# Maxima of a cross-attention kernel: rounds of four in four banks instead of three in three

## The chip, the cores and the metric

The kernel runs on one core of one Trainium2 chip. The metric is the device time of one execution in microseconds (us): the median of three runs of the kernel before is 1541.65 us, and they lie between 1541.1 and 1544.61 us. The engines are called PE (TensorE, matrix products), PEld (its weight loads), DVE (VectorE), ACT (ScalarE), POOL (GpSimd) and SP (which issues most of the transfers).

## The reference, cut to what matters

The inputs are x (4 x 2048 x 640) and ctx (4 x 154 x 384). The last four rows of each ctx are the tokens `ca`, the first 150 the keys.

```
query = x @ Wq;  keyt = enc @ Wk;  valt = enc @ Wv
hs = _mha(query, keyt, valt)                          # 8 heads, 2048 x 150
ca_q1 = jnp.einsum('btc,th->bch', ca, Wq_ca)          # 384 x 640
ca_q1 = ca_q1[:, indices, :]                          # 384 rows spread over 2048
ca_hs1 = _mha(ca_q1, residual, residual)              # 384 distinct rows against all 2048 rows of x
ca_q2 = ca_hs1 @ Wq
ca_hs2 = _mha(ca_q2, ca @ Wk_ca, ca @ Wv_ca)
out = (hs + ca_hs2) @ Wout + b_out + residual
```

The change is in `ca_hs1`. Its scores are a product of rank 4 in each head: `g` = x times `Wq_ca` by head (4 rows a head) against the 384 columns of `ca`. Softmax needs the greatest score of each of the 384 rows, and the kernel computes it over all 2048 positions before it computes any exponential.

## The kernel before

The program loops over four batches, and each goes through the same stages, written out by hand for each engine; semaphores join the engines.

**Stage of products.** x comes in four chunks of 512 rows, each in five column blocks, so 20 pieces m = 0..19. For each piece PE transposes four 128x128 blocks into a PSUM bank (`turn_x`), ACT copies the bank to `xt` (`copy_x`), and PE multiplies the copy with `gyw_b` (`products`, 8 matmuls as the profile shows them). After the five pieces of a chunk, ACT and DVE take the sums (`copy_y`), DVE splits the token columns (`split_g`), PE turns them (`turn_g`) and ACT copies them to `g` (`copy_g`). The pieces and the turned `g` alternate between the two banks of `ps_t` (`piece_bank`, `piece_free`). In the same stage PE also computes the first chunk's queries for the main attention, 75 matmuls of 512 columns, in portions of `Q0_FILL` per step and then of `Q0_SPLIT`, `Q0_TURNED` and `Q0_TRIPLE` (`queries0`).

**Maxima.** A unit (`max_unit`) is one matmul of 12 or 28 rows by 512 columns: one group r (0..3, two heads, rows from 32 r) of one of three blocks of 128 rows against one chunk. Each fills a bank of `ps_s`, and DVE reduces that bank to 128 maxima (`unit_maxima`, L1311). There are 48 units for the even heads (phase 0) and 48 for the odd heads (phase 1). `UNITS_EARLY` says how many units of phase 1 run in the stage of products beside the 48 of phase 0: 6 in each of chunks 0 and 1, which makes 60. They come in 20 groups of three (`TRIPLES`, then the last four groups with five query matmuls between them). With three banks, unit u waits until DVE has reduced unit u - 3. The PE stream is in order: behind a unit that waits, everything of PE waits. `TRIPLES[m]` puts a group after the transposes, after the products or after the queries of step m.

**First softmax phase.** After the 60 units DVE puts the maxima in place (`place_maxima`), PE turns them into bank 2 of `ps_s` (`turn_ca`, T_BANK), and DVE copies that to `ca_mat` (`take_ca`, L1327). Then come 16 steps: scores (`scores`, rows 0 to 63 into `ps_w`, rows 64 to 127 into `ps_t`), ACT's exponentials (L1124) and weighings (`weigh`). The other 36 units stand between the scores, `UNITS_STEP` of them a step, in three banks.

The second softmax phase and 16 tiles of the main attention follow, and are the same in both kernels.

Of the kernel before, what the change touches and what calls it, by code (L numbers as in the profile page):

```python
# [21 lines left out]
P = 128  # L22
# [101 lines left out]
M_BANKS = 3  # L124
# [4 lines left out]
UNITS_EARLY = 6  # L129


def unit_order():

    early, late = [], []
    for q in range(CHUNKS):
        units = [(ct, r) for ct in range(CT) for r in range(GROUPS)]
        early += [(0, q, ct, r) for ct, r in units]
        n = UNITS_EARLY if q + 2 < CHUNKS else 0
        early += [(1, q, ct, r) for ct, r in units[:n]]
        late += [(1, q, ct, r) for ct, r in units[n:]]  # L140
    return early + late, len(early)
# [4 lines left out]
TRIPLES = {8: (AFTER_TURNED, AFTER_QUERIES), 9: (AFTER_PRODUCTS,), 10: (AFTER_TURNED,), 11: (AFTER_TURNED,), 12: (AFTER_TURNED,),  # L146
           13: (AFTER_TURNED, AFTER_QUERIES), 14: (AFTER_PRODUCTS,), 15: (AFTER_TURNED,), 16: (AFTER_TURNED,), 17: (AFTER_TURNED,),
           18: (AFTER_TURNED, AFTER_QUERIES), 19: (AFTER_PRODUCTS,), 20: (AFTER_TURNED,)}
UNITS_BEFORE_SPLIT = 12
Y_SHARED = (0,)  # L150
Q0_FILL = [0] * 6 + [3, 0, 4, 3, 2, 1, 2, 4, 4, 2, 2, 3, 4, 4, 1]
Q0_ENDS = (6, 12, 17)
Q0_SPLIT, Q0_TURNED, Q0_TRIPLE = 9, 3, 5
UNITS_STEP = [3, 2, 3, 2, 3, 2, 2, 3, 2, 3, 2, 3, 2, 2, 0, 0]
# [65 lines left out]
def cross_attention(nc, x, ctx, Wq, Wk, Wv, Wq_ca, Wk_ca, Wv_ca, Wout, b_out,  # L220
                    c_ident, c_head_of, c_block_of, c_pick, c_rem_of, c_last_row, c_hi_lo, c_spread, out):
    with ExitStack() as stack:
# [167 lines left out]
        piece_bank = {piece: ps_t[:, n % 2, :] for n, piece in enumerate(PIECES)}  # L390
# [115 lines left out]
        def _(pe):  # L506
# [80 lines left out]
            for b in range(B):  # L587
# [16 lines left out]
                for n in V_ORDER:  # L604
                    if n == 1:
                        pe.wait_ge(ca_base_ready, PHASES * (b + 1))
                    if n == V_ORDER[-1]:
                        pe.wait_ge(xc_in[0], 16 * (b * XC_LOADS + 1))
                        turn_x(0, 0, piece_bank[("x", 0)], gx_turned)
# [35 lines left out]
                def turn_g(i):  # L645
# [3 lines left out]
                    for t in range(ST):  # L649
                        last = turned(piece_bank[("g", i)][:, t * P:(t + 1) * P], gst[:, t, :, :].rearrange("p h k -> p (h k)"))  # L650
# [39 lines left out]
                for m in range(GX + 1):  # L690
                    if 0 < m < GX:
# [22 lines left out]
                    triple(AFTER_PRODUCTS)  # L714
# [3 lines left out]
                    triple(AFTER_QUERIES)  # L718
# [5 lines left out]
                for u in range(first, PHASE0_UNITS, M_BANKS):  # L724
                    max_units(u, M_BANKS)
                    if u + M_BANKS < PHASE0_UNITS:
                        queries0(done, Q0_TRIPLE)
                        done += Q0_TRIPLE
# [245 lines left out]
        def _(act):  # L974
# [22 lines left out]
            for b in range(B):  # L997
# [12 lines left out]
                def copy_x(m):  # L1010
# [10 lines left out]
                    nc.scalar.activation(xt[:, xt_slot(m), :], piece_bank[("x", m)], copy).then_inc(xt_copied, 1)  # L1021
# [157 lines left out]
        def _(dve):  # L1179
# [77 lines left out]
            for b in range(B):  # L1257
# [82 lines left out]
                for i in range(1, CHUNKS):  # L1340
                    chunk = per_chunk + (UNITS_EARLY if i < CHUNKS - 1 else 0)
# [177 lines left out]
```

## Time and profile before

| | |
|---|---|
| median of three runs | 1541.65 us (1541.1 to 1544.61) |
| the profiled execution | 1540.79 us |
| its span, first to last instruction | 1539.0 us |
| mean granted TensorE clock | 0.996 |
| busy: PE, PEld, DVE, ACT | 97%, 81%, 51%, 40% |
| PE's share of the chain that ended last | 91% |

Busy shares are averages over unlike stages. PE's rows overlap each other, and their ends are modelled; what a piece of work costs PE is the distance from its start to the start of what comes next. An "idle before" value says how long the engine stood still, and for whom. A wait that sits between two matmuls of one group is inside the group's duration, so a group's second number is to be compared with that of its like.

### The profile page before, as it was taken

The numbers are of one execution on the slowest core, as the hardware profiler recorded it, in microseconds if no ns is written. First come the engines' busy times: TensorE is split into PE (matmuls) and PEld (weight loads), VectorE is DVE, ScalarE is ACT, GpSimd is POOL, SyncE is SP. The second block draws the span as 40 slices with busy tenths as digits, with TensorE's granted clock in tenths as the row PEclk, the third lists the DMA queues.
The fourth block names the chain that finished last, engine by engine and source line by source line (L and its number), as shares of the span: only waits on it lengthen the run. The fifth ranks groups of instructions, "written<-read, shape, count | busy, mean of one in ns | idle before, by whom it ended". The sixth has DMA issues, their size and how long they took to land.

```text
span 1539.0 us, 24550 instructions
## 1 busy us (share of the span) xinstructions
PE 1499.8 (97%) x10306; PEld 1247.5 (81%) x10306; DVE 791.1 (51%) x1595; ACT 620.0 (40%) x1310; POOL 2.8 (0%) x12
## 2 busy tenths in 40 slices
PE   6999999999999999999999999999999999999998
PEld 4764699999976489999987549999998745999998
DVE  5686445344468453443447826335345882443533
ACT  1428723233243862332333584233333368333322
POOL 0000000000000000000000000000000000000000
PEclk9999999999999999999999999999999999999999
DMA  6530011130253001131035200204004510021101
GB/s 241 205 136 35 3 54 70 55 114 26 89 170 130 1 16 48 66 111 54 35 111 182 88 1 20 82 28 156 18 35 155 180 38 1 20 95 57 61 18 43
DMA packets 46680, 117.28 MB, mean 76 GB/s; under 512 B 3661, under 2 KB 5317, under 8 KB 45019
## 3 DMA queue, kind: packets, MB, share of 16 engines
q1 hardware_dynamic: 37036, 93.91, 17.4%
q10 hardware_dynamic: 9535, 21.80, 3.7%
q8 instruction: 82, 1.34, 0.3%
q14 instruction: 27, 0.22, 0.0%
HBM read 77.33 MB, written 39.17 MB: 76 GB/s over the span
## 4 chain that ended last, share of the span: by engine, by line
PE 91%; DVE 4%; ACT 2%; issue 2%; DMA 0%; SPq 0%
PE ps_w L508 46%; PE ps_s L508 19%; PE ps_t L508 16%; PE ps_t L518 5%; PE ps_w L518 3%; DVE unit_max L1311 2%; ACT work L1124 1%; PE ps_s L518 1%; ACT ot L1038 0%; DMA y_all<-in_L_xattn_Wv_ca_dram 0%; DVE ca_mat L1327 0%; DVE ot L1423 0%; ACT ot L1107 0%; DVE xt_l L1337 0%; ACT work L1021 0%
## 5 line engine op out<-in xcount | busy, mean ns | idle before, releaser
L508 PE MATMUL ps_w<-wo_h,ot 128*128 128x320 f32 x1280 | 310.4, 314 | 0.6 <-DVE ot L1423 0.6
L1311 DVE TENSOR_REDUCE unit_max<-ps_s 128x1 f32<-128x512 f32 x384 | 240.6, 683 | 53.1 <-PE ps_s L508 52.2
L1094 ACT ACTIVATE work<-ps_s,neg_max 128x150 f32<-128x150 f32 x512 | 152.5, 403 | 223.4 <-DVE neg_max L1369 223.4
L508 PEld LDWEIGHTS ps_w<-wo_h,ot 128*128 128x128 f32 x1280 | 220.3, 188 | 0.9 <-DVE ot L1423 0.9
L508 PE MATMUL ps_w<-wo_l,ot 128*128 128x320 f32 x640 | 197.4, 308 | 0.0
L508 PEld LDWEIGHTS ps_w<-v_all,work 120*128 120x128 f32 x1280 | 170.3, 190 | 3.0 <-issue 2.5
L508 PE MATMUL ps_w<-v_all,work 120*128 120x162 f32 (+1 forms) x1280 | 171.3, 288 | 0.0
L1365 DVE TENSOR_REDUCE neg_max<-ps_s 128x6 f32<-128x900 f32 x64 | 70.1, 1095 | 165.2 <-PE ps_s L508 165.2
L508 PE MATMUL ps_s<-keys_h,qt_h 128*128 128x300 f32 (+1 forms) x448 | 140.0, 313 | 0.0
L508 PE MATMUL ps_s<-keys_h,qt_l 128*128 128x300 f32 (+1 forms) x448 | 131.5, 294 | 0.0
L508 PE MATMUL ps_s<-keys_l,qt_h 128*128 128x300 f32 (+1 forms) x448 | 131.1, 293 | 0.0
L1434 DVE TENSOR_TENSOR work<-ps_w,xc 128x320 f32<-128x320 f32 x128 | 62.4, 488 | 130.9 <-PE ps_w L508 130.9
L1391 DVE TENSOR_TENSOR qt_l<-ps_t,qt_h 128x512 fp32r<-128x512 f32 x60 | 41.5, 691 | 162.1 <-ACT qt_h L1076 162.1
L508 PEld LDWEIGHTS ps_w<-wo_l,ot 128*128 128x128 f32 x640 | 120.4, 188 | 0.2
L508 PE MATMUL ps_t<-xt_h,wq_h 128*128 128x512 f32 x300 | 119.3, 398 | 0.4
L1124 ACT ACTIVATE work<-ps_w 128x768 f32<-128x768 f32 x128 | 104.2, 814 | 35.2 <-PE ps_t L508 20.8
L508 PE MATMUL ps_t<-xt_h,wq_l 128*128 128x512 f32 x300 | 117.7, 392 | 0.0
L508 PE MATMUL ps_t<-xt_l,wq_h 128*128 128x512 f32 x300 | 116.6, 389 | 0.0
L1107 ACT ACTIVATE ot<-ps_w 128x640 fp32r<-128x640 f32 x64 | 45.0, 704 | 175.1 <-PE ps_w L518 175.1
L508 PE MATMUL ps_w<-work,y_all 128*32 128x384 f32 x1024 | 109.1, 498 | 0.1
L508 PEld LDWEIGHTS ps_s<-keys_h,qt_h 128*128 128x128 f32 x448 | 84.9, 189 | 25.5 <-issue 25.0
L1076 ACT ACTIVATE qt_h<-ps_t 128x512 fp32r<-128x512 f32 x60 | 35.9, 598 | 169.3 <-PE ps_t L508 169.3
(163 smaller groups left out, 2346.9 us busy)
## 6 DMA issues: line engine op xcount, KB each, us to landing
xc<-in_x_dram SPq DMA_DIRECT2D x32, 1280.0 KB, 6.5
out_dram<-work ACTq DMA_DIRECT2D x64, 320.0 KB, 2.2
xt_all<-work SPq DMA_DIRECT2D x60, 256.0 KB, 2.2
xt_l<-xt_all SPq DMA_DIRECT2D x12, 1280.0 KB, 5.6
y_all<-in_L_xattn_Wk_dram SPq DMA_DIRECT2D x4, 960.0 KB
y_all<-in_L_xattn_Wv_dram SPq DMA_DIRECT2D x4, 960.0 KB
pick<-pick_all SPq DMA_DIRECT2D x16, 194.0 KB
xc<-in_L_xattn_Wq_dram SPq DMA_DIRECT2D x1, 1600.0 KB, 10.5
```

Source lines behind the costliest of these rows:

```text
L508: return nc.tensor.matmul(out, lhs, rhs, start=start, stop=stop, skip_group_check=True)
L518: return nc.tensor.transpose(out, in_, ident[0:k, 0:k])
L1076: nc.scalar.activation(dst, ps_t[:, bank_of(use), :], copy).then_inc(t_high, 1)
L1094: return nc.scalar.activation(probs[:, h * KEYS:(h + 1) * KEYS], ps_s[:, bank, c * KEYS:(c + 1) * KEYS], exp, bias=neg_max[:, s % 2, h:h + ...
L1107: nc.scalar.activation(ot_h[:, s % 2, :], ot_psum, copy).then_inc(ot_high, 1)
L1124: nc.scalar.activation(e_buf[n % E_BUFS][:, 2 * p:2 * p + 2, :], score_banks[p], exp, scale=SCALE).then_inc(w_ready, 1)
L1311: v.tensor_reduce(unit_max[:, a, n, q:q + 1], bank, AX_X, ALU.max).then_inc(max_free, 1)
L1365: v.tensor_reduce(neg_max[:, s % 2, 0:6].rearrange("p (a h) -> p a h", a=2), ps_s[:, 0:2, 0:3 * KEYS].rearrange("p a (h k) -> p a h k", h= ...
L1391: v.tensor_tensor(dst, ps_t[:, bank_of(use), :], high_part, ALU.subtract).then_inc(t_free[bank_of(use)], 1)
L1434: v.tensor_tensor(o_tile[:, s % 2, cols], out_banks[half], xc[:, c % 2 * ST + t, cols], ALU.add).then_inc((ya_ready, y_ready)[half], 1)
```

## The change

The maxima of the stage of products run four at a time in four banks: the three of `ps_s` and the second bank of `ps_t`. That bank had been half of the pair in which the turned pieces alternate, so all pieces now use the first bank of `ps_t`, and each waits for the copy of the one before. `UNITS_EARLY` becomes 4 and 4, so 56 units run in the stage of products, in 14 rounds of four (11 by `ROUNDS`, then three with five queries between), and 40 are left for the first softmax phase, which keeps its three banks. The queries' portions are dealt out anew: the three at m = 6, which ran ahead of the products, go to later steps, and 14 instead of 9 stand between the last round and `turn_ca(0)`. Unit 56, the first of the softmax phase, now falls into bank 2, the one that `turn_ca` has just filled, and so waits for `ca_ready`; the number of throwaway matmuls (`UNREAD`) is as before, with another bank.

```diff
-M_BANKS = 3
+M_BANKS, G_BANKS = 3, 4
-UNITS_EARLY = 6
+UNITS_EARLY = [4, 4, 0, 0]
-        n = UNITS_EARLY if q + 2 < CHUNKS else 0
+        n = UNITS_EARLY[q]
-TRIPLES = {8: (AFTER_TURNED, AFTER_QUERIES), 9: (AFTER_PRODUCTS,), 10: (AFTER_TURNED,), 11: (AFTER_TURNED,), 12: (AFTER_TURNED,),
-           13: (AFTER_TURNED, AFTER_QUERIES), 14: (AFTER_PRODUCTS,), 15: (AFTER_TURNED,), 16: (AFTER_TURNED,), 17: (AFTER_TURNED,),
-           18: (AFTER_TURNED, AFTER_QUERIES), 19: (AFTER_PRODUCTS,), 20: (AFTER_TURNED,)}
+ROUNDS = {8: AFTER_TURNED, 9: AFTER_TURNED, 10: AFTER_TURNED, 12: AFTER_PRODUCTS, 13: AFTER_TURNED,
+          14: AFTER_TURNED, 15: AFTER_TURNED, 17: AFTER_PRODUCTS, 18: AFTER_TURNED, 19: AFTER_TURNED, 20: AFTER_TURNED}
+UNIT_BANK = [u % (G_BANKS if u < PHASE0_UNITS else M_BANKS) for u in range(PHASES * UNITS)]
+UNIT_PREVIOUS = [max((w for w in range(u) if UNIT_BANK[w] == UNIT_BANK[u]), default=None) for u in range(PHASES * UNITS)]
-Q0_FILL = [0] * 6 + [3, 0, 4, 3, 2, 1, 2, 4, 4, 2, 2, 3, 4, 4, 1]
-Q0_ENDS = (6, 12, 17)
-Q0_SPLIT, Q0_TURNED, Q0_TRIPLE = 9, 3, 5
-UNITS_STEP = [3, 2, 3, 2, 3, 2, 2, 3, 2, 3, 2, 3, 2, 2, 0, 0]
+Q0_FILL = [0] * 7 + [4, 3, 2, 2, 2, 2, 4, 3, 2, 3, 3, 4, 3, 2]
+Q0_ENDS = (12, 17)
+Q0_SPLIT, Q0_TURNED, Q0_ROUND = 9, 3, 5
+UNITS_STEP = [3, 3, 3, 2, 3, 3, 3, 2, 3, 3, 3, 3, 3, 1, 0, 0]
-        piece_bank = {piece: ps_t[:, n % 2, :] for n, piece in enumerate(PIECES)}
+        piece_bank = ps_t[:, 0, :]
+        unit_banks = [ps_s[:, 0, :], ps_s[:, 1, :], ps_s[:, 2, :], ps_t[:, 1, :]]
                 def piece_free(piece):
-                    if n >= 2:
-                        kind, old = PIECES[n - 2]
+                    if n:
+                        kind, old = PIECES[n - 1]
                 def max_unit(u):
-                    if u >= M_BANKS:
-                        pe.wait_ge(max_free, b * PHASES * UNITS + u - M_BANKS + 1)
+                    if u >= G_BANKS:
+                        pe.wait_ge(max_free, b * PHASES * UNITS + UNIT_PREVIOUS[u] + 1)
-                queries0(done, 2 * Q0_TRIPLE)
+                queries0(done, KT * Q0_MM)
                 turn_ca(0)
-                queries0(done + 2 * Q0_TRIPLE, KT * Q0_MM)
-                    mm(ps_s[:, T_BANK, :], wq_h[:, n, 0:P], xt_h[:, n, :], True, True)
+                    mm(unit_banks[UNIT_BANK[PHASE0_UNITS + 2]], wq_h[:, n, 0:P], xt_h[:, n, :], True, True)
-                    chunk = per_chunk + (UNITS_EARLY if i < CHUNKS - 1 else 0)
+                    chunk = per_chunk + UNITS_EARLY[i - 1]
```

## Rows read from the trace of the kernel before

**Rows 1.** The page: the chain that ended last, by engine.
```profile
PE 91%; DVE 4%; ACT 2%; issue 2%; DMA 0%; SPq 0%
```
**Rows 2.** Busy time by window: us, PE, PEld, DVE, ACT, POOL, clock, DMA.
```profile
438.60:490.20 51.60, 50.34 (x297) 35.94 (x297) 42.38 (x76) 13.93 (x26) 0.00 (x0) 1.00 0.44 148
...
494.30:515.90 21.60, 21.60 (x188) 8.84 (x187) 18.96 (x31) 18.62 (x26) 0.00 (x0) 1.00 0.02 8
...
849.50:852.90 3.40, 3.40 (x13) 2.92 (x13) 1.93 (x6) 0.98 (x2) 0.00 (x0) 0.51 0.90 322
```
**Rows 3.** PE in order of time, second batch: start, duration, instruction, count, idle before.
```profile
437.21 0.60 PE L518 MATMUL ps_t<-ident,gst 128*128 128x128 f32 x4
437.65 0.60 PE L518 MATMUL ps_t<-ident,xc 128*128 128x128 f32 x4
438.59 0.50 PE L508 MATMUL ps_s<-ot,ca_mat 12*128 12x512 f32 x3 [0.34 <-ACT ot L1038]
439.02 1.10 PE L508 MATMUL ps_w<-gyw_b,work 128*128 128x56 f32 x8
...
441.04 0.50 PE L508 MATMUL ps_s<-ot,ca_mat 12*128 12x512 f32 x3
...
442.92 1.09 PE L508 MATMUL ps_s<-ot,ca_mat 12*128 12x512 f32 x3
...
445.81 1.10 PE L508 MATMUL ps_w<-gyw_b,work 128*128 128x56 f32 x8
...
459.70 0.60 PE L518 MATMUL ps_t<-ident,xc 128*128 128x128 f32 x4
460.23 0.50 PE L508 MATMUL ps_s<-ot,ca_mat 12*128 12x512 f32 x3
460.66 1.10 PE L508 MATMUL ps_w<-gyw_b,work 128*128 128x56 f32 x8
```
**Rows 4.** DVE in order of time: six reductions behind two groups of units.
```profile
441.58 3.76 DVE L1311 TENSOR_REDUCE unit_max<-ps_s 128x1 f32<-128x512 f32 x6 [0.60 <-PE ps_s L508]
```
**Rows 5.** ACT in order of time: the copy of g and the copy of a chunk's sums.
```profile
437.85 0.60 ACT L1038 ACTIVATE ot<-ps_t 128x512 fp32r<-128x512 f32 x1 [0.70 <-PE ps_t L518]
...
446.94 0.98 ACT L1033 ACTIVATE y_all<-ps_w 128x448 f32<-128x448 f32 x2 [0.97 <-PE ps_w L508]
```
**Rows 6.** PE in order of time: the end of the stage and the first scores.
```profile
480.46 0.50 PE L508 MATMUL ps_s<-ot,ca_mat 12*128 12x512 f32 x3
...
482.25 1.14 PE L508 MATMUL ps_s<-ot,ca_mat 12*128 12x512 f32 x3
...
489.76 0.49 PE L518 MATMUL ps_s<-ident,cst 128*128 128x128 f32 x3
490.18 0.50 PE L508 MATMUL ps_s<-ot,ca_mat 28*128 28x512 f32 x2
490.90 0.44 PE L508 MATMUL ps_w<-ca_mat,ot 32*128 32x384 f32 x2 [0.22 <-DVE ca_mat L1327]
```
**Rows 7.** PE in order of time: steps 6 and 7 of the stage of products.
```profile
433.48 0.48 PE L508 MATMUL ps_w<-xt_h,wq_h 128*128 128x512 f32 x1
...
435.00 1.07 PE L508 MATMUL ps_w<-gyw_b,work 128*128 128x56 f32 x8 [0.57 <-DVE y_all L1294]
435.91 0.61 PE L518 MATMUL ps_t<-ident,xc 128*128 128x128 f32 x4
436.36 1.02 PE L508 MATMUL ps_w<-gyw_b,work 128*128 128x84 f32 x8
```
**Rows 8.** DVE in order of time in the first softmax phase.
```profile
495.59 7.87 DVE L1311 TENSOR_REDUCE unit_max<-ps_s 128x1 f32<-128x512 f32 x12 [0.78 <-PE ps_s L508]
```
**Rows 9.** PE in order of time: the start of a step of the first softmax phase.
```profile
495.06 0.50 PE L508 MATMUL ps_s<-ot,ca_mat 28*128 28x512 f32 x1
495.06 0.44 PE L508 MATMUL ps_w<-ca_mat,ot 32*128 32x384 f32 x2
495.07 0.49 PE L508 MATMUL ps_s<-ot,ca_mat 28*128 28x512 f32 x1
```

More of the change, by code:

```diff
@@ L411, in unit @@
         def unit(u):
-            return (*UNIT_ORDER[u], ps_s[:, u % M_BANKS, :])
+            return (*UNIT_ORDER[u], unit_banks[UNIT_BANK[u]])
         @block.sync
@@ L608, in _ @@
                         pe.wait_ge(xc_in[0], 16 * (b * XC_LOADS + 1))
-                        turn_x(0, 0, piece_bank[("x", 0)], gx_turned)
+                        turn_x(0, 0, piece_bank, gx_turned)
                     at, lo, hi = KR * n % KEYS, V_HEADS[n][0] * DH, (V_HEADS[n][-1] + 1) * DH
@@ L649, in turn_g @@
                     for t in range(ST):
-                        last = turned(piece_bank[("g", i)][:, t * P:(t + 1) * P], gst[:, t, :, :].rearrange("p h k -> p (h k)"))
+                        last = turned(piece_bank[:, t * P:(t + 1) * P], gst[:, t, :, :].rearrange("p h k -> p (h k)"))
                     last.then_inc(gt_full, 1)
@@ L697, in _, with a_round @@
                         piece_free(("x", m))
-                        turn_x(i % 2, kt, piece_bank[("x", m)], gx_turned)
-                    def triple(place):
+                        turn_x(i % 2, kt, piece_bank, gx_turned)
+                    def a_round(place):
                         nonlocal first
-                        if place in TRIPLES.get(m, ()):
-                            max_units(first, M_BANKS)
-                            first += M_BANKS
+                        if ROUNDS.get(m) == place:
+                            max_units(first, G_BANKS)
+                            first += G_BANKS
                     if m in Q0_ENDS:
                         queries0(done, Q0_FILL[m])
-                    triple(AFTER_TURNED)
+                    a_round(AFTER_TURNED)
                     if m >= 1:
@@ L713, in _ @@
                             turn_g(i - 1)
-                    triple(AFTER_PRODUCTS)
+                    a_round(AFTER_PRODUCTS)
                     if m not in Q0_ENDS:
@@ L717, in _ @@
                     done += Q0_FILL[m]
-                    triple(AFTER_QUERIES)
+                    a_round(AFTER_QUERIES)
                 queries0(done, Q0_SPLIT)
@@ L723, in _ @@
                 done += Q0_TURNED
[L724 to L728, printed above, removed]
+                for u in range(first, PHASE0_UNITS, G_BANKS):
+                    max_units(u, G_BANKS)
+                    if u + G_BANKS < PHASE0_UNITS:
+                        queries0(done, Q0_ROUND)
+                        done += Q0_ROUND
                 def turn_ca(a):
@@ L1020, in copy_x @@
                             act.wait_ge(xt_stored[old % XT_RING], 16 * (b * XT_STORES[old % XT_RING] + XT_NTH[old]))
-                    nc.scalar.activation(xt[:, xt_slot(m), :], piece_bank[("x", m)], copy).then_inc(xt_copied, 1)
+                    nc.scalar.activation(xt[:, xt_slot(m), :], piece_bank, copy).then_inc(xt_copied, 1)
                 for m in range(VT_HALF - 1):
@@ L1037, in copy_g @@
                     act.wait_ge(gt_full, b * CHUNKS + i + 1)
-                    nc.scalar.activation(g[:, i * CHUNK:(i + 1) * CHUNK], piece_bank[("g", i)], copy).then_inc(g_ready, 1)
+                    nc.scalar.activation(g[:, i * CHUNK:(i + 1) * CHUNK], piece_bank, copy).then_inc(g_ready, 1)
                 def q0_highs(j):
```

## The prediction

> **What bounds the kernel now.** I read the chain of waits first: PE makes 91% of it [rows 1]. Then busy time by window. The stage of products of the second batch runs from its first unit to the first unit of the softmax phase, 51.6 us: PE is busy in 50.34 of it and DVE in 42.38 [rows 2]. So DVE has some 9 us of air in the stage and isn't its bound as a whole; PE is, with stalls that its busy time partly hides, since a stall inside a group lengthens the row. These I took from the order of time. PE's stream is fixed, so a unit whose bank is still being reduced holds back everything behind it. A free group of three takes 0.43 us (438.59 to 439.02, 460.23 to 460.66), three concurrent passes, while one whose third unit waits lasts 1.09 instead of 0.50 [rows 3]. In the first softmax phase 13 steps take 21.6 us, 1.66 each, with DVE busy 18.96 and ACT 18.62 [rows 2]: PE, ACT and DVE are all nearly full there.
>
> **The gain: fewer passes.** 20 groups become 14 rounds. That four units cost what three do is not shown in this stage, but in the softmax phase a unit, two scores and another unit start within 0.01 us (495.06, 495.06, 495.07) on four groups of rows [rows 9], so I take 0.43 for a round of four. With its switches a group costs a bit more: from transposes to products it is 0.45 without a group (435.91 to 436.36 [rows 7]) and 0.96 with one (459.70 to 460.66 [rows 3]), so 0.51. Six fewer: -3.06 us a batch. From below, the bare pass, it would be -2.58.
>
> First the row: three units, 0.43 us on PE; their reductions, six in 3.76 us, or (3.76 - 0.68) / 5 = 0.61 each on DVE, 1.8 for three and 2.4 for four [rows 3, 4] (0.68 is a reduction's own mean by the page). The Trainium skill, TensorEngine Tiling (Array Packing), sections Tiling Modes and PSUM Bottleneck, says that four tiles of 32 rows work independently, and that tiling speeds up TensorE but not the emptying of PSUM. The trace agrees for three. By its first half alone the sum would be the second rival's; its second half speaks against this change.
>
> **Queries.** The three at m = 6 are free today: they stand in a wait for DVE's copy of the sums, which lasts until 435.00 whatever PE does [rows 7]. Moved behind it they cost 3 x 0.23 = +0.69 a batch (0.23 is the distance between two of them, by their starts in the stage). The hole that they leave costs nothing more.
>
> **Stalls.** When may a round start? The first reduction starts 0.54 after the unit (441.04 to 441.58 [rows 3, 4]), each next one 0.605 later, and a bank is free 0.05 after its reduction of 0.68 ends (the third ends at 441.58 + 1.21 + 0.68 = 443.47, and the third unit of the group of 1.09 starts 0.59 late, at 443.51). So the four banks are free 1.27, 1.87, 2.48 and 3.07 us after a round's start, if DVE was idle. Between two rounds PE has products 0.91 (435.00 to 435.91 [rows 7]), transposes 0.53 (459.70 to 460.23 [rows 3]) and two, three or four queries (0.55, 0.81, 1.04), plus the pass, 0.43. I walked through the 14 rounds so:
> - m = 8 to 9, three queries: 0.43 + 0.91 + 0.81 + 0.53 = 2.68, so the fourth unit waits 0.39. m = 9 to 10: 0.27.
> - No round at m = 11. The products of chunk 2 wait for the copy of the sums: it starts 1.13 after the last products' start (445.81 to 446.94) and takes 0.98 [rows 3, 5]. With 0.13 until PE goes on (the copy of g ends at 438.45, the unit starts at 438.59), they start 2.24 after the last products, where PE would be there after 0.91 + 0.55 + 0.49 = 1.95: 0.29, at m = 11 and m = 16. Today a group covers this.
> - m = 12, a round behind `turn_g`; it covers the copy of g, but with one bank the transposes of m = 13 now wait for that copy: 437.21 to 437.85, 0.60, 0.05, or 1.29 after the turning's start [rows 3, 5], against 0.88 for the turning and the round: 0.41. Their round follows 1.29 - 0.45 + 0.53 = 1.37 after the one before. Its fourth bank is free only at 3.07: a stall of **1.70 us**. DVE had nothing to do in the four microseconds ahead of it. The same pair stands at m = 17 and 18: 2 x (0.41 + 1.70) = 4.22.
> - m = 14 and 19: 0.12 each, m = 15: 0.28, m = 20 (three queries, no transposes): 0.71.
> - The three last rounds, with five queries between, as far apart as now: 480.46 to 482.25 is 1.79 [rows 6], and the fourth bank is free after 3.04: 1.25, then 0.62. Fourteen queries instead of nine then cover DVE's last reductions, so `turn_ca` waits for PE's own work.
>
> The sum is 0.39 + 0.27 + 0.58 + 4.22 + 0.24 + 0.28 + 0.71 + 1.87 = 8.56 us a batch. Before, read the same way: three waits for g, each 0.94 from transposes to unit instead of 0.50 [rows 3], 1.32; three groups of 1.09 instead of 0.50 [rows 3], 1.77; one of 0.81, 0.32; two in the tail, 1.14 instead of 0.50 [rows 6], 1.28; four small ones, 0.29. Together 4.98. So stalls grow by +3.58, and the stage by -3.06 + 0.69 + 3.58 = **+1.21 us a batch**.
>
> **One bank for the pieces.** At m = 2 to 6 the transposes start each 1.29 after the last. The copy starts 0.64 after the transposes, takes 0.60 and is seen 0.05 later (as with g [rows 3, 5]): 1.29 too. The cover is exact, so I take +0.10 for a lost early weight load here and there, between 0 and 0.5.
>
> **Unit 56.** Today two units run under DVE's copy to `ca_mat` (490.18), and the scores start when it ends (490.90) [rows 6]. Unit 56 is now in the copied bank, so both units start at its end, on rows 0 to 63, and the first scores, on the same rows, come a pass later: +0.29, between 0.2 and 0.4. The exponentials and the first weighing follow them and shift.
>
> **First softmax phase.** Four more units: DVE +4 x 0.605 = 2.42 at most. Steps of three need 1.82 on DVE against 1.66 now [rows 2, 4]; 35 units in the 13 steps need 21.2 of the present 21.6. Before, a run of 12 reductions without a gap (7.87 [rows 8]) made its steps no longer, because three banks let PE be ahead. The last five full steps, 15 units, need 9.1 against 8.3: +0.8, of which the banks swallow part; and unit 56's shift puts more leading units on the scores' rows. I take +0.6, between 0.1 and 1.3.
>
> **The sum.** 1.21 + 0.10 + 0.29 + 0.60 = 2.20 a batch, 8.8 for four. Nothing after the phase changes. Against the profiled execution: 1540.79 + 8.8 = 1549.6 us; the median of the runs is 0.86 above that execution, so **1550.5 us**. The bounds (stage 0.8, if half of the small stalls don't show, to 1.7, with the bare pass; the others as given) are 1.1 and 3.9 a batch: 1546 to 1557.
>
> **Rivals.** (1) *The clock.* In the third batch of this execution PE ran at 0.51 of its clock, the lower level (1.2 GHz), for 3.4 us in the stage of products [rows 2]; it costs at most half of that, 1.7 us. More and longer stalls may bring two to four more of these: 1550.5 + 3.4 to 6.8, 1554 to 1557. For it: the one fall stands in this stage. Against it: three batches of four have none. The Trainium skill, TensorE: Matmul & The Clock Gate, section A second HAM failure mode: psum-queue depth-cycling, tells of PE pausing between groups as PSUM banks come round until the clock swings; this trace shows one such fall.
> (2) *The rounds don't wait more than now* (the other side). If the rounds found their banks free as often as the triples do, the stalls stay at 4.98, the stage gains 3.06 - 0.69 = 2.37, and with 0.99 for the rest a batch gains 1.38: 1541.65 - 5.5 = 1536.1 us. The point is 6.4 us of stalls a batch: below it the kernel is faster. The two stalls of 1.70 decide; without both it would come out near 1537. For it: DVE has air in the stage. Against it: the air lies elsewhere, since two rounds 1.37 apart can't have four reductions of 0.605 between them.
> (3) *No difference*: half of the grown stalls don't show and the softmax phase hides its four units: 1.21 - 1.79 + 0.1 + 0.2 + 0.1 = -0.2 a batch, about 1541.
> (4) *It doesn't do what it says*: if the fourth unit were not concurrent, each round costs 0.22 more, 14 x 0.22 = 3.1 a batch, and the time is 1562. The rows of four starts speak against it.
>
> **How the numbers follow.** The forecast (1546 to 1554) has 0.63, more falls of the clock 0.13, the second rival 0.12, no difference 0.09, the last 0.03. Some 0.2% is what a measurement of this kernel tells from no change, 3 us. Faster 0.12, same 0.09, slower 0.79. The range, 1543.5 to 1556.5, leaves out the second and last rivals and part of the third.
>
> **What would show it.** PE in order of time after the change: rounds of four at 0.43 where free; behind each `turn_g` of chunks 1 and 2 a round, and then one of about 2.1 us instead of 0.5; DVE idle some 4 us ahead of it; two groups near 1.7 in the tail; `turn_ca` 54.9 to 55.3 us after the first transposes of m = 7 (before: 435.91 to 489.76, 53.85 [rows 6, 7]); the scores 0.29 later behind the copy; 13 weighings in 22.2. The prediction is wrong if the rounds at m = 13 and 18 are short, or the softmax phase grows by DVE's whole 2.42.

## The result, and the profile after

The changed kernel takes 1585.11 us (median of four runs, 1578.09 to 1595.19), the kernel before 1542.65 beside it (1541.1 to 1544.61): a ratio of 1.028, 95% interval 1.022 to 1.034. So it is slower, as forecast, but by 42 us and not by 9, and outside the range given. The profiled execution has a span of 1583.7 us against 1539.0.

First the page of the kernel after: the chain that ended last, by engine, and the granted clock in 40 slices.

```profile
PE 89%; DVE 6%; ACT 2%; issue 1%; DMA 1%; SPq 0%
...
PEclk9979999999987999999999999999999899999999
```

PE still sets the end, with DVE at 6% instead of 4% [rows 1]; that is the longer wait for reductions. The new thing is in the clock's line, which is all nines for the kernel before: the stage of products of the first, second and fourth batch shows a 7 or an 8 (the third batch's low time is spread over two slices and stays a 9). The windows say how much. This is busy time by window from the first products of a batch to `turn_ca(0)` (columns as in [rows 2]); first two batches of the kernel before:

```profile
53.70:116.40 62.70, 60.50 (x383) 45.63 (x384) 46.59 (x85) 21.35 (x39) 0.00 (x0) 1.00 0.45 154
427.10:489.80 62.70, 60.53 (x384) 45.63 (x385) 46.64 (x85) 21.28 (x39) 0.00 (x0) 1.00 0.46 154
```

and all four of the kernel after:

```profile
54.80:127.20 72.40, 69.40 (x379) 53.36 (x380) 44.01 (x81) 21.62 (x39) 0.00 (x0) 0.86 0.40 134
439.80:516.40 76.60, 73.61 (x380) 56.16 (x381) 43.92 (x81) 21.59 (x39) 0.00 (x0) 0.80 0.37 126
828.90:898.90 70.00, 66.85 (x379) 50.49 (x380) 43.86 (x81) 21.69 (x39) 0.00 (x0) 0.90 0.41 138
1211.50:1280.80 69.30, 66.32 (x380) 50.71 (x381) 43.93 (x81) 21.61 (x39) 0.00 (x0) 0.90 0.41 140
```

PE has fewer instructions and stays busy longer: its work is stretched. A clock of 0.80 over 76.6 us means (1 - 0.80) x 2 x 76.6 = 30.6 us at the lower of the two levels, 1.2 GHz. Added up from the single steps of the clock in the trace, the four stretches have 78.5 us at that level, where the kernel before has 3.4. "Low time" below is this sum. The cost is in the length of the stages, from PE's order of time (us; low time in brackets; in the kernel before the third batch's second line is 52.74 with 3.4 low). The last column is the first batch of e5, a run described below: the changed kernel with unread matmuls in its two longest waits, in which the clock doesn't fall in this batch and the two waits are as long as before.

| stage, per batch | before | after, batches 1 to 4 | after at full clock (e5, first batch) |
|---|---|---|---|
| first products to first unit | 11.54 | 13.90 (3.4), 13.89 (3.4), 13.89 (3.4), 12.40 (0) | 12.39 |
| first unit to `turn_ca(0)` | 51.16 | 58.52 (17.1), 62.75 (27.3), 56.07 (10.2), 56.90 (13.7) | 51.54 |
| to the first weighing | 4.53 | 4.86 | 4.87 |
| first softmax phase | 24.10 | 25.69 | 25.68 |
| rest, batches 1 to 3 | 282.0 | 282.0 | 282.1 |

Against the last column, what the waits and the moved work cost at full clock is 0.85 + 0.38 + 0.34 + 1.58 = 3.15 a batch, 12.6 us. What the clock costs is 6.98 + 11.21 + 4.53 + 5.36 in the second line and 3 x 1.50 in the first, 32.6 us, or 0.41 us for each us of low time; the kernel before has 1.6 of the kind. 12.6 + 32.6 - 1.6 = 43.6, and 1 us more stands ahead of the first stage: the 44.7 by which the spans differ.

**The waits that were forecast are there.** PE of the kernel after in order of time, fourth batch, in a stretch at full clock, around the round behind `turn_g` of chunk 1 (this answers to [rows 3]):

```profile
1235.46 0.60 PE L520 MATMUL ps_t<-ident,gst 128*128 128x128 f32 x4
...
1235.99 0.51 PE L510 MATMUL ps_s<-ot,ca_mat 28*128 28x512 f32 x3
1236.00 0.50 PE L510 MATMUL ps_t<-ot,ca_mat 28*128 28x512 f32 x1
...
1236.75 0.66 PE L520 MATMUL ps_t<-ident,xc 128*128 128x128 f32 x4 [0.25 <-ACT ot L1039]
...
1237.33 1.63 PE L510 MATMUL ps_s<-ot,ca_mat 12*128 12x512 f32 x3
1239.06 0.49 PE L510 MATMUL ps_t<-ot,ca_mat 12*128 12x512 f32 x1
1239.48 1.10 PE L510 MATMUL ps_w<-gyw_b,work 128*128 128x56 f32 x8
```

The four units of the first round start within 0.01 us. Those of the second start at 0, 0.53, 1.13 and 1.73 us, and PE goes on after 2.15. DVE beside it, in order of time (this answers to [rows 4]):

```profile
1236.52 1.89 DVE L1312 TENSOR_REDUCE unit_max<-ps_s 128x1 f32<-128x512 f32 x3 [3.55 <-PE ps_t L510]
1238.33 0.68 DVE L1312 TENSOR_REDUCE unit_max<-ps_t 128x1 f32<-128x512 f32 x1
1238.92 0.68 DVE L1333 TENSOR_TENSOR qt_l<-ps_w,qt_h 128x512 fp32r<-128x512 f32 x1
1239.52 1.87 DVE L1312 TENSOR_REDUCE unit_max<-ps_s 128x1 f32<-128x512 f32 x3
```

DVE stood still for 3.55 us and then got eight reductions almost at once. And this is PE at the lower level, later in the same batch: products followed by three queries.

```profile
1260.49 2.00 PE L510 MATMUL ps_w<-gyw_b,work 128*128 128x84 f32 x8
...
1262.22 0.77 PE L510 MATMUL ps_w<-xt_l,wq_h 128*128 128x512 f32 x1
...
1262.79 0.63 PE L510 MATMUL ps_w<-xt_h,wq_l 128*128 128x512 f32 x1
...
1263.22 0.63 PE L510 MATMUL ps_w<-xt_h,wq_h 128*128 128x512 f32 x1
```

The products take 2.00 by their row instead of 1.02 [rows 7], and two queries start 0.43 apart instead of 0.23.

**Where the clock falls.** There are twelve falls in the four stages. Three stand behind the products of m = 6, 3.4 us each. Seven stand behind the second round of a pair (m = 13 or 18; one of them starts while its last unit waits), and they hold 61.4 us of the 78.5; of the eight such rounds only one has none behind it. Two stand in the tail, 3.4 each. One of the seven, PE in order of time up to the fall at 1255.5 and the window behind it; the other is the longest:

```profile
1253.19 1.62 PE L510 MATMUL ps_s<-ot,ca_mat 12*128 12x512 f32 x3
1254.91 0.50 PE L510 MATMUL ps_t<-ot,ca_mat 12*128 12x512 f32 x1
1255.34 0.96 PE L510 MATMUL ps_w<-gyw_b,work 128*128 128x56 f32 x4
```

```profile
1255.50:1269.20 13.70, 13.70 (x50) 10.67 (x51) 7.97 (x15) 1.57 (x3) 0.00 (x0) 0.50 0.42 137
487.50:504.60 17.10, 17.10 (x58) 13.05 (x59) 9.19 (x17) 2.17 (x4) 0.00 (x0) 0.50 0.37 124
```

PE is busy through both, and the clock doesn't rise.

The scores behind `turn_ca(0)` answer to [rows 6]:

```profile
1280.77 0.49 PE L520 MATMUL ps_s<-ident,cst 128*128 128x128 f32 x3
...
1282.00 0.50 PE L510 MATMUL ps_s<-ot,ca_mat 28*128 28x512 f32 x2 [0.74 <-DVE ca_mat L1328]
1282.13 0.44 PE L510 MATMUL ps_t<-ca_mat,ot 32*128 32x384 f32 x2
...
1282.31 0.36 PE L510 MATMUL ps_w<-ca_mat,ot 32*128 32x384 f32 x2
```

Unit 56 waits for DVE's copy, and the scores on its rows of PE come behind it. The first softmax phase, second batch, as a window:

```profile
521.30:547.00 25.70, 25.45 (x213) 9.60 (x212) 22.69 (x39) 20.94 (x29) 0.00 (x0) 1.00 0.01 2
```

### The profile page after: what moved, and what is told of

It reads as the page before. It is cut to its first block, busy times and chain, and to the rows that moved or that the text cites. A ratio compares the mean times of both kernels' runs of the same rounds, so it can differ in the third digit from the quotient of the medians.

```text
span 1583.7 us, 24554 instructions
## 1 busy us (share of the span) xinstructions
PE 1537.8 (97%) x10306; PEld 1273.5 (80%) x10306; DVE 788.1 (50%) x1595; ACT 621.9 (39%) x1310; POOL 2.8 (0%) x12
## 3 DMA queue, kind: packets, MB, share of 16 engines
q8 instruction: 82, 1.34, 0.3%
## 4 chain that ended last, share of the span: by engine, by line
PE 89%; DVE 6%; ACT 2%; issue 1%; DMA 1%; SPq 0%
PE ps_w L510 47%; PE ps_s L510 16%; PE ps_t L510 16%; PE ps_t L520 6%; DVE unit_max L1312 4%; PE ps_w L520 3%; ACT work L1125 1%; PE ps_s L520 1%; DMA xc<-in_L_xattn_Wout_dram 1%; DMA y_all<-in_L_xattn_Wv_ca_dram 0%; ACT y_all L1034 0%; DVE ca_mat L1328 0%; DVE ot L1424 0%; ACT ot L1108 0%; DVE wq_l L1204 0%
## 5 line engine op out<-in xcount | busy, mean ns | idle before, releaser
L1312 DVE TENSOR_REDUCE unit_max<-ps_s 128x1 f32<-128x512 f32 x328 | 204.8, 683 | 90.9 <-PE ps_t L510 69.7
L510 PEld LDWEIGHTS ps_w<-gyw_b,work 128*128 128x128 f32 x640 | 87.7, 211 | 22.6 <-issue 12.3
```

What stands on the lines that cost most here:

```text
L510: return nc.tensor.matmul(out, lhs, rhs, start=start, stop=stop, skip_group_check=True)
L1312: v.tensor_reduce(unit_max[:, a, n, q:q + 1], bank, AX_X, ALU.max).then_inc(max_free, 1)
```

## The experiments

Two theories stood after the result. **The waits' length**: the 42 us are PE's waits, only longer than forecast. **The clock**: the waits are as forecast and, with the softmax phase, cost some 13 us, and the clock falls behind them. Within the second it was open which waits bring the falls: the pause at m = 6, from which the three queries were taken, the two of 1.7 us behind `turn_g` (m = 13 and 18), or all the short ones together. Low time and lengths are of the profiled execution, for the four batches; the ratio is to runs of the kernel before on the same chip.

| | median us | ratio (95%) | low time us | first unit to `turn_ca(0)` |
|---|---|---|---|---|
| after | 1585.11 | 1.028 (1.022 to 1.034) | 78.5 | 56.07 to 62.75 |
| e1, throwaways in nearly all waits | 1555.84 | 1.0075 (1.006 to 1.010) | 0 | 52.15 |
| e5, at m = 13 and 18 only | 1561.98 | 1.012 (1.009 to 1.015) | 20.5 | 51.54 to 54.55 |
| e9, everywhere but there | 1590.26 | 1.030 (1.028 to 1.032) | 88.8 | 60.59 to 63.82 |
| e3, queries back at m = 6 | 1585.98 | 1.028 (1.026 to 1.030) | 75.1 | 56.93 to 61.20 |
| e4, rounds after the queries | 1580.44 | 1.024 (1.020 to 1.028) | 68.3 | 56.04 to 61.24 |
| e12, rounds after the products | 1558.54 | 1.009 (1.008 to 1.011) | 37.5 | 51.07 to 58.06 |
| e6, e1 with other steps of the softmax phase | 1553.95 (one run) | | 0 | 52.12 to 52.16 |
| e2, before without queries at m = 6 | 1545.0 | 1.0017 (1.0002 to 1.003) | 6.8 | 51.19 to 51.22 |
| e11, before with throwaways | 1549.76 | 1.0045 (1.003 to 1.006) | 3.4 | 53.31 to 54.96 |
| e7, 60 units in 15 rounds | 1542.99 | 1.0011 (0.9998 to 1.002) | 12.6 | 49.90 to 52.81 |
| e8, e7 with six throwaways | 1542.68 | 1.0006 (0.9996 to 1.002) | 0 | 50.36 |
| e13, 60 units, rounds behind g | 1548.81 | 1.0036 (1.002 to 1.005) | 37.5 | 50.99 to 55.74 |
| e10, e13 with twelve throwaways | 1540.34 | 0.9987 (0.998 to 0.9996) | 0 | 50.05 |

**Are the 42 us waits or clock? (e1)** The changed kernel with 26 matmuls a batch whose results nobody reads, put where PE would stand still: six where units 16 and 32 start their rounds (m = 13 and 18), five ahead of the products of m = 6, nine at other rounds. They write the bank that the next unit overwrites, and nothing of the computation is left out.

```diff
+THROWN = {4: 1, 16: 6, 32: 6, 40: 2, 48: 4, 52: 2}
+THROWN_6 = 5
+    if n == G_BANKS and first in THROWN:
+        if first >= G_BANKS:
+            pe.wait_ge(max_free, b * PHASES * UNITS + UNIT_PREVIOUS[first] + 1)
+        for k in range(THROWN[first]):
+            mm(unit_banks[UNIT_BANK[first]], wq_h[:, k % KT, 0:P], wq_h[:, k % KT, 0:CHUNK], True, True)
...                                            # THROWN_6 likewise, ahead of the products of m = 6
```

> The kernel after, with throwaway matmuls of 512 columns in PE's known waits: five at m = 6 ahead of the products, six ahead of the rounds at m = 13 and 18, one at m = 9, two at m = 20, four and two in the tail; 26 a batch, 104 in all, 0.23 us each, all where PE stood still. Theory A (the waits let the TensorE clock fall, and the low clock is most of the loss): time at the low clock, 79 us in the span after, falls below 25 us, and the time to 1554 to 1564 us. Theory B (the waits themselves are the loss, the clock is a companion): the waits stay as long as they are, so 1585 us, at most 3 us more.

Measured: 1555.84 us with more work on PE, 29.3 less than without. The window of the first and second batch, and PE in order of time around the second round of the pair:

```profile
55.70:120.30 64.60, 63.54 (x406) 49.91 (x407) 44.08 (x81) 21.66 (x39) 0.00 (x0) 1.00 0.45 150
433.00:497.50 64.50, 63.46 (x406) 49.79 (x407) 44.07 (x81) 21.59 (x39) 0.00 (x0) 1.00 0.45 150
```

```profile
458.48 0.66 PE L522 MATMUL ps_t<-ident,xc 128*128 128x128 f32 x4 [0.26 <-ACT ot L1049]
...
459.00 1.66 PE L512 MATMUL ps_s<-wq_h 128*128 128x512 f32 x6
...
460.59 0.50 PE L512 MATMUL ps_s<-ot,ca_mat 12*128 12x512 f32 x3
460.79 0.49 PE L512 MATMUL ps_t<-ot,ca_mat 12*128 12x512 f32 x1
461.21 1.10 PE L512 MATMUL ps_w<-gyw_b,work 128*128 128x56 f32 x8
```

The six throwaways fill the wait and shorten nothing: from the transposes of m = 13 to the next products it is 2.73 us in both kernels (458.48 to 461.21; 1236.75 to 1239.48 above). So these waits are still there, and the 29 us are the clock. The first theory falls. What stays, 13 us, is the change at full clock and the throwaways' own cost. That cost is not nothing: the stage takes 52.15 here and 51.54 in the first batch of e5, which has throwaways at m = 13 and 18 alone. In the tail, from the first of the three last rounds to the fourteen queries, it is 6.22 us (1242.34 to 1248.56) against 5.85 in e5, and from the transposes of m = 10 to the products 1.45 against 1.19. These throwaways outlast the waits they stand in or let the units start later, 0.6 us a batch, 2.4 in all; so the clock is worth somewhat more than 29 us, and the table above takes e5's batch and not e1.

**Which waits? (e5, e9)** The same throwaways in two parts.

```diff
-THROWN = {4: 1, 16: 6, 32: 6, 40: 2, 48: 4, 52: 2}
-THROWN_6 = 5
+THROWN = {16: 6, 32: 6}                    # e5
+THROWN_6 = 0
+THROWN = {4: 1, 40: 2, 48: 4, 52: 2}       # e9
+THROWN_6 = 5
```

> The kernel after with throwaway matmuls only ahead of the rounds at m = 13 and 18, six each, 12 a batch. If those two waits of 1.7 us are what the clock falls behind: low time from 79 us to below 25 us, 1555 to 1562 us, as with all 26. If every wait counts alike: about half of the gain, 1567 to 1575 us.

> The kernel after with throwaway matmuls in every wait but the two of 1.7 us at m = 13 and 18: five at m = 6, one at m = 9, two at m = 20, four and two in the tail, 14 a batch. All 26 gave 1555.8 us and no low clock in the stage, the pairs alone 1562.0 and 20 us of it. If the two long waits are enough for the clock to fall: low time in the four stages 40 us or more, 1570 to 1580 us. If it is the sum of waits over some microseconds that counts, and either half helps: below 30 us, 1558 to 1568 us.

The first batch and the fourth of e5, then of e9:

```profile
53.70:117.60 63.90, 61.30 (x391) 47.73 (x392) 43.88 (x81) 21.64 (x39) 0.00 (x0) 1.00 0.45 152
...
1187.40:1255.90 68.50, 65.87 (x392) 51.15 (x393) 43.87 (x81) 21.64 (x39) 0.00 (x0) 0.93 0.42 141
```

```profile
54.50:127.50 73.00, 71.44 (x393) 54.66 (x394) 43.98 (x81) 21.67 (x39) 0.00 (x0) 0.86 0.39 133
...
1211.30:1287.50 76.20, 74.67 (x393) 57.20 (x394) 44.09 (x81) 21.62 (x39) 0.00 (x0) 0.82 0.38 127
```

Twelve throwaways a batch in the two waits of 1.7 us bring back 23 of the 29 us, and no fall is left behind a pair: three of e5's four are in the tail, one behind m = 6. Fourteen everywhere else bring back nothing: the falls at m = 6 are gone, but behind each of the eight second rounds of a pair the clock is low for 10.2 to 17.1 us, and 1590 us is above both expectations. PE is busy for 98% of e9's windows and the clock is still at 0.82 and 0.86: the share of busy time doesn't tell of the falls, since a unit's row counts its waits. A shorter wait can bring a fall as well: in the tail, where e5's three falls stand, the fourth unit waits 1.25 us. That the two waits of 1.7 us are needed for most of the low time is shown; which length is enough is not.

**The pause at m = 6 (e2, e3).** The two kernels with the three queries taken away and given back.

```diff
-Q0_FILL = [0] * 6 + [3, 0, 4, 3, 2, 1, 2, 4, 4, 2, 2, 3, 4, 4, 1]      # before
+Q0_FILL = [0] * 6 + [0, 3, 4, 3, 2, 1, 2, 4, 4, 2, 2, 3, 4, 4, 1]      # e2
-Q0_FILL = [0] * 7 + [4, 3, 2, 2, 2, 2, 4, 3, 2, 3, 3, 4, 3, 2]         # after
+Q0_FILL = [0] * 6 + [3, 1, 3, 2, 2, 2, 2, 4, 3, 2, 3, 3, 4, 3, 2]      # e3
...                                            # Q0_ENDS: 6 taken out in e2, put back in e3
```

> The kernel before with one part of the change alone: the three queries of m = 6 run at m = 7, behind the products and the turning of g. By the sum of the prediction they cost 0.69 us a batch and cover 0.4 of the wait for g: +1 to +3 us, 1543 to 1545 us. Theory A1 (the pause of 1.2 us that this opens at m = 6 is what the clock falls behind): clock falls ahead of the first unit of a batch, 1.5 us for each, 1546 to 1551 us. Theory A2 (the falls come from the pauses at the rounds): no fall there, 1543 to 1545 us.

> The kernel after with that part undone: three queries back at m = 6 ahead of the products, one at m = 7. Theory A1 (the pause at m = 6 starts most of the low clock): low time falls from 79 us by more than half, 1555 to 1565 us. Theory A2 (the pauses at the rounds do): only the falls ahead of the first unit go (10 us of low time, 4.5 us) and 0.69 x 4 of queries, 1576 to 1580 us.

In e2 the clock falls twice, both times ahead of the first unit, for 3.4 us each (13.46 instead of 11.83 there). In e3 no fall is left ahead of the first unit, but the stage behind it has 75.1 us of them. So this pause makes the single falls at the head of the batches, 1.5 us each, and not the rest; e3's median of 1585.98 is above what either theory gave, since the stage has more low time than before. At full clock e3's head is 12.38 and that of the kernel after 12.40: the queries given back gain nothing, since the transposes of m = 8 now wait for the copy of g in any case.

**The order of the rounds (e4, e12).** The six rounds at m = 13 to 15 and 18 to 20 stand later in their steps, so that the two of a pair lie further apart.

```diff
-ROUNDS = {8: AFTER_TURNED, 9: AFTER_TURNED, 10: AFTER_TURNED, 12: AFTER_PRODUCTS, 13: AFTER_TURNED,
-          14: AFTER_TURNED, 15: AFTER_TURNED, 17: AFTER_PRODUCTS, 18: AFTER_TURNED, 19: AFTER_TURNED, 20: AFTER_TURNED}
+    # e4:  13, 14, 15, 18, 19, 20: AFTER_QUERIES
+    # e12: 13, 14, 15, 18, 19, 20: AFTER_PRODUCTS
```

> The kernel after with the rounds of m = 13, 14, 15 and of 18, 19, 20 behind the queries of their steps instead of behind the transposes. The two waits of 1.7 us a batch go, and one of about 1.6 us comes ahead of the last turning of g: at an unchanged clock -2 us a batch, 1577 us. Theory A2 (these pauses make the clock fall): low time goes from 79 us to under 40 us, and the time to 1555 to 1568 us. Theory A1: 1574 to 1579 us.

> The kernel after, no throwaways, with the rounds of m = 13, 14, 15, 18, 19 and 20 behind the products of their steps. The two waits of 1.7 us shrink to about 0.75 each and aren't replaced: the queries find DVE's low part about ready, unlike with the rounds behind the queries, where a wait of 1.4 us on it took their place. If only waits of more than a microsecond let the clock fall: low time in the stages 0 to 25 us, 1550 to 1560 us. If shorter waits of the same kind do as well: above 40 us, 1570 us or more.

e4 exchanged one wait for another. PE in its fourth batch:

```profile
1230.74 1.00 PE L510 MATMUL ps_w<-gyw_b,work 128*128 128x56 f32 x8
...
1233.15 0.51 PE L510 MATMUL ps_w<-xt_h,wq_h 128*128 128x512 f32 x1 [1.42 <-DVE qt_l L1333]
```

The queries now stand still for 1.42 us, because DVE makes the low parts of the queries before (`qt_l`) behind the four reductions of the round. The low time stays at 68.3 us, and the time, 1580.44 (1571.62 to 1587.68), is as expected by neither theory. In e12 the rounds come behind the products, where no such queue forms; its fourth batch:

```profile
1216.29 0.51 PE L510 MATMUL ps_s<-ot,ca_mat 28*128 28x512 f32 x3
...
1218.47 0.80 PE L510 MATMUL ps_s<-ot,ca_mat 12*128 12x512 f32 x3
...
1219.37 0.54 PE L510 MATMUL ps_t<-ot,ca_mat 12*128 12x512 f32 x1
```

Two rounds 2.18 us apart instead of 1.34, and the second's three units last 0.80 instead of 1.63; its fourth unit waits 0.90 us. The time is 1558.54, 27 us less than that of the kernel after, without a throwaway: the order of six rounds was worth most of the loss. But 37.5 us of low time are left, more than the 0 to 25 expected of long waits alone. Counted over the four batches, four falls stand behind second rounds like the one shown (its own from 1219.67 on) and hold 23.9 us, two in the tail hold 10.2 and one at m = 6 3.4. So a wait of 0.90 us in such a round can bring a fall too. The first batch alone has 23.9 us of low time, and why it differs I can't say.

**The softmax phase and unit 56 (e6).** e1, with unit 56 in another bank than the turned one, and another distribution of the 40 units.

```diff
-UNIT_BANK = [u % (G_BANKS if u < PHASE0_UNITS else M_BANKS) for u in range(PHASES * UNITS)]
+UNIT_BANK = [u % G_BANKS if u < PHASE0_UNITS else (u + 1) % M_BANKS for u in range(PHASES * UNITS)]
-UNITS_STEP = [3, 3, 3, 2, 3, 3, 3, 2, 3, 3, 3, 3, 3, 1, 0, 0]
+UNITS_STEP = [3, 2, 3, 3, 3, 3, 3, 2, 3, 3, 3, 3, 3, 1, 0, 0]
...                                            # the waits for unit 56's bank and for the last units' follow
```

> The first kernel with throwaways (1555.8 us), with two changes of the softmax phase: unit 56 in bank 0 instead of the bank just turned, and two units instead of three in the second and five times three behind it. If the bank is what costs between the turning and the first weighing: 4.86 us there goes back to 4.53. If the two leading steps of three, with DVE behind, break the exponentials' ring: the step of 2.45 us goes and the way from the first weighing to the second turning falls from 25.7 to at most 24.9 us. Rival: DVE's four more reductions are the cost wherever they stand, 25.5 to 25.8 us. Time 1551 to 1555 us.

From `turn_ca(0)` to the first weighing it is 4.54, as before the change (4.53) and 0.33 less than in e1: unit 56's bank is the whole of that term. The softmax phase stays at 25.78 (e1: 25.70). So the growth doesn't hang on where these units stand. It goes with the four units: e10, which has four banks and rounds of four in the stage of products but 36 units here, takes 24.23 against 24.10 before. Whether it is their reductions on DVE or their passes on PE was not told apart.

**Throwaways in the kernel before (e11).** Two ahead of five groups. Its stages have one fall, so the expectation was that at most 1.6 us is to be gained.

```diff
+THROWN = {6: 2, 24: 2, 42: 2, 51: 2, 57: 2}
...                                            # run as in e1
```

> The kernel before with two throwaway matmuls in each of its five waits of 0.6 us a batch. The one fall of the clock in its profile cost 1.6 us; if such falls come from those waits, low time in the stages goes to nothing and the time falls by up to 1.6 us, 1540 to 1541.7 us, with runs closer together. If the throwaways lengthen the waits (three units then start a little later): +0.5 us a batch at most, 1543 us.

The stage grew by 2.2 us a batch and the time to 1549.76, more than expected, and one fall is left. A throwaway must wait for the bank before it runs, and then the group's first unit, DVE's reduction of it and the units behind start later: in the second batch the first group with throwaways starts 1.45 us after the products instead of 0.95 and lasts 0.59 instead of 1.09, so that nothing is gained or lost there, but the group behind it lasts 1.12 instead of 0.61. Where PE's waits are short, filling them costs.

**What four at a time is worth with shorter waits (e7, e8, e13, e10).** All 60 units in the stage, in 15 rounds of four, with the later rounds behind the products (from m = 13 in e7 and e8, from m = 12 in e13 and e10) and the softmax phase as before the change.

```diff
-UNITS_EARLY = [4, 4, 0, 0]
+UNITS_EARLY = [8, 4, 0, 0]
+ROUNDS = {8: AFTER_TURNED, 9: AFTER_TURNED, 10: AFTER_TURNED, 11: AFTER_TURNED, 12: AFTER_TURNED, 13: AFTER_PRODUCTS,
+          14: AFTER_PRODUCTS, 15: AFTER_PRODUCTS, 16: AFTER_PRODUCTS, 18: AFTER_PRODUCTS, 19: AFTER_PRODUCTS, 20: AFTER_PRODUCTS}
+    # e13, e10: 12 behind the products too, and 17 instead of 16, so that a round covers the copy of g
-Q0_FILL = [0] * 7 + [4, 3, 2, 2, 2, 2, 4, 3, 2, 3, 3, 4, 3, 2]
+Q0_FILL = [0] * 6 + [3, 4, 2, 2, 2, 1, 1, 4, 4, 2, 2, 3, 4, 3, 3]
+Q0_ENDS = (6, 12, 17)
+Q0_SPLIT = 11
+UNITS_STEP = [3, 2, 3, 2, 3, 2, 2, 3, 2, 3, 2, 3, 2, 2, 0, 0]      # as before the change
+THROWN = {52: 4, 56: 2}                    # e8
+THROWN = {20: 3, 36: 3, 52: 4, 56: 2}      # e10
```

> Four banks and rounds of four, but 60 units in the stage of products as before (eight and four of the second phase), in 15 rounds with no two close together, three queries back at m = 6, and the softmax phase as before with 36 units. No throwaways. By the prediction's terms, at full clock: 15 passes instead of 20 is -2.6 us a batch, stalls 5.8 instead of 5.0, one bank for the pieces +0.2: 1535 to 1538 us. If rounds of four and one bank make the clock fall however they are laid out: low time 40 to 80 us, 0.4 us lost for each, 1552 to 1570 us. If only the long waits do: 1535 to 1541 us.

> The kernel with 60 units in 15 rounds, and four and two throwaway matmuls in the waits of the last two rounds. At full clock as without them, 1535 to 1538 us; if the waits of the tail are what the clock falls behind, it gives that and the one without gives 5 us or more above it; if not, the two are equal.

> The kernel of 60 units with two rounds behind the turnings of g (1540.3 us with 12 throwaways a batch), without any throwaway. At full clock it would be equal or 0.5 us a batch faster, 1538 to 1540.5 us; with the clock falling behind its waits of 0.75, 1.25 and 0.6 us it would be 1542 to 1548 us, and the low time shows which wait it is.

> The kernel with 60 units in 15 rounds and throwaways in the tail (1542.7 us), with the rounds of m = 12 and 16 moved behind the turning of g at m = 12 and 17, where PE waited 0.84 us for the copy of g, and three throwaways each ahead of the rounds at m = 13 and 18, which now wait about 0.75 us. The waits for the copy shrink to 0.4 us and a wait of 0.6 us in a round goes, for two new ones of 0.75: -0.3 to -0.6 us a batch, 1540 to 1542 us. Rival: queries at m = 13 and 18 wait for DVE's low part behind the four reductions, and nothing is gained: 1542 to 1544 us.

e7 and e8 miss their 1535 to 1538 us: 1542.99 and 1542.68, the same as the kernel before. Where e7's clock doesn't fall, the stage takes 49.90, 1.26 less than before the change, but the way to the first unit takes 12.40, 0.86 more, and the way from `turn_ca(0)` through the softmax phase 0.2 more: 0.2 us a batch is gained and not 1.6. Six throwaways a batch keep e8 free of low time and lengthen the stage to 50.36, and the two kernels come out equal.

The first batch of e10, then the first and third of e13:

```profile
54.90:117.30 62.40, 60.76 (x395) 47.48 (x395) 45.64 (x85) 21.59 (x39) 0.00 (x0) 1.00 0.46 155
```

```profile
54.10:117.50 63.40, 61.33 (x383) 47.41 (x383) 45.56 (x85) 21.67 (x39) 0.00 (x0) 0.97 0.45 153
...
802.80:871.00 68.20, 66.22 (x384) 51.47 (x385) 46.22 (x85) 21.69 (x39) 0.00 (x0) 0.87 0.42 142
```

Between the first unit and `turn_ca(0)` e10 takes 50.05 us, 1.1 less than the kernel before; up to the first unit it takes 12.40 against 11.54, 0.86 more, which is the one bank for the pieces and g; 0.2 more lies behind `turn_ca(0)`. The sum is zero at full clock, and the kernel before has one fall of 1.6 us. Measured: 0.9987, interval 0.998 to 0.9996, about 2 us faster. e13, the same without its twelve throwaways a batch, is 8.5 us slower at 37.5 us of low time, though none of its waits is longer than 1.25 us. Four of its six falls, 27.3 us, stand behind rounds at m = 13 or 18 whose fourth unit waits 0.9 us, and two in the tail. e10 is the only kernel here that is faster than the one before.

## Why the prediction was right or wrong

The direction was right, with its reason: the waits grow by more than the saved passes are worth, though the larger part of the loss at full clock, 1.58 of 3.15 us a batch, is the softmax phase. The size failed at one step, the price of the clock; beside it one term was put at nothing and one was mis-sized.

**The step that failed is the price in the first rival.** The prediction saw the clock's fall, named it as a rival and priced it at "two to four more of these", 3.4 to 6.8 us, from the one fall of [rows 2]. The runs show eleven falls more, some of them 6.8 to 17.1 us long, 75 us more of low time, over 20 times that one, and 31 us. The premise was that each fall stands alone, as in the kernel before, and costs at most half of 3.4. The two new waits of 1.7 us a batch, the longest of the stage, are in the prediction's sum of stalls but not in this price: 61.4 us of the low time start behind them, with them filled 20.5 us are left (e5), with all others filled 88.8 (e9). "Against it: three batches of four have none" was an argument from a stage that didn't have these waits. The Trainium skill, TensorE: Matmul & The Clock Gate, section A second HAM failure mode: psum-queue depth-cycling, tells of short idles between groups behind which the clock swings between its two levels; the traces agree, with 78.5 us at the lower level here. Taken at its word it would have made the rival the forecast; it gives no price, and only the runs do.

**The waits, at full clock.** Fourth batch, as forecast and as found: the fourth unit at m = 9 waits 0.39, found 0.42; at m = 10 0.27, 0.23; the products of m = 11 0.29, 0.3; the transposes of m = 13 0.41, 0.33 (1236.75 - 1235.99 - 0.43); the round behind them 2.1, 2.15; m = 14 0.12, 0.12; m = 15 0.28, 0.30; m = 20 0.71, 0.74 (e5's first batch); the two in the tail 1.25 and 0.62, found 1.24 and 0.61. DVE's pause ahead of the pair is 3.55, "some 4". A free round of four in the fourth batch, and then the round of the tail that waits longest:

```profile
1223.87 0.50 PE L510 MATMUL ps_s<-ot,ca_mat 12*128 12x512 f32 x3
...
1224.30 1.10 PE L510 MATMUL ps_w<-gyw_b,work 128*128 128x56 f32 x8
...
1273.39 1.14 PE L510 MATMUL ps_s<-ot,ca_mat 12*128 12x512 f32 x3
1274.63 0.49 PE L510 MATMUL ps_t<-ot,ca_mat 12*128 12x512 f32 x1
1275.06 0.50 PE L510 MATMUL ps_w<-xt_h,wq_l 128*128 128x512 f32 x1
```

The free round takes 0.43 (to 1224.30), so rival 4 falls. The other takes 1.67, and its fourth unit starts 1.24 after its first. Rival 2 falls too: the rounds at m = 13 and 18 do wait.

**The stage's sum** at full clock is +1.23 a batch (0.85 + 0.38) where 1.21 + 0.10 was said; from the first transposes of m = 7 to `turn_ca` it is 54.85, where 54.9 to 55.3 was given. Within it two terms are off, in opposite directions. One bank was taken at +0.10 under an "exact" cover; the transposes of m = 2 to 6 come 1.31 to 1.43 apart instead of 1.29, +0.25 by m = 6. The queries of m = 6 didn't cost their +0.69 by themselves: e3 gives them back and gains nothing, since the wait of the transposes of m = 8 for the copy of g takes the same time.

**The hole at m = 6** was put at nothing ("The hole that they leave costs nothing more"). At an unchanged clock that holds, but three of the four holes brought a fall of 3.4 us, 1.50 us each, 4.5 in all; with the queries back (e3) none of these is left.

**Unit 56** +0.29, found +0.34, and 0.33 by e6. Right, and by the mechanism named.

**The first softmax phase** +0.60, found +1.58, outside the 0.1 to 1.3 given. This is the mis-sized term. The step was "of which the banks swallow part": the full steps of three were priced on DVE alone, against an average step. Found: step 2 grows from 1.90 to 2.45, step 5 from 1.56 to 1.95 and step 11 from 1.62 to 2.08, and the first 13 weighings take 23.4 and not 22.2. e6 shifts units between the steps and gains nothing. What decides how much of the 2.42 shows was not isolated.

**The sum at full clock** is 1.23 + 0.34 + 1.58 = 3.15 a batch, within the bounds of 1.1 to 3.9. e1, with its throwaways' own 2.4 us in it, has 1555.8 us, inside the range of 1543.5 to 1556.5. The range was right for the kernel that was priced, and the clock took it from there to 1585.

## What to carry to other kernels

A wait of PE is not priced by its length alone: where a change makes the longest wait of a stretch with many short ones, price the whole stretch at the lower clock as the bad case, here 0.41 us for each us. Look at the granted clock by window before anything else when a kernel is slower than its instructions say. Fill only waits that are there and long, with work that doesn't delay what the next engine waits for, and first see whether another order takes them away (e12 gained 27 us so, the throwaways 29).

## What the runs showed of the hardware

- The clock went to its lower level (a granted clock of 0.5) behind waits of 1.7 us in the stage of products, in a stretch where the row of PE says 96% busy (69.40 of 72.40 us), and stayed there for most of what followed in some batches: 10.2 to 27.3 us a batch behind the same instructions. With the two waits filled (e5) the stage took 54.55 us at most. Waits of 0.9 us in a round of e12 and e13 had falls behind them too.
- At that level products start 1.73 us before what follows instead of 0.91, and four queries take 1.85 instead of 1.01. Per us of low time the stages lose 0.41, not 0.5; part of the reason is that waits for DVE go meanwhile: the fourth unit of the round at m = 20 waits 0.74 us at full clock (e5's first batch) and none in the fourth batch of the kernel after, where the clock is low.
- Throwaway matmuls in a wait hold the clock: 26 a batch are worth 29 us (e1), 12 a batch 23 us (e5) or 8.5 us (e10 against e13), and 14 in the wrong places nothing (e9). Where they delay the next units they cost: 0.6 us a batch in e1, 0.46 in e8 against e7, 2.2 in e11.
- Four matmuls on four groups of rows start within 0.01 us and cost 0.43 together, as three do; DVE's reductions of the four banks take 4 x 0.605 = 2.42. The Trainium skill, TensorEngine Tiling (Array Packing), section PSUM Bottleneck, says that tiling speeds up TensorE but not the emptying of PSUM; these numbers agree.

Open are the length, or the sum of lengths, of waits at which the clock falls: no run changed one wait in steps. Open too is why one batch of a run has three times the low time of another with the same instructions.
